# Relative-position attention on one core: query tile 0 split into two halves for the scores and the logits

## What is computed

```python
idx = clip(key - query, -64, 64) + 64
rk, rv = embK[idx], embV[idx]
q, k, v = proj(Wq, bq), proj(Wk, bk), proj(Wv, bv)          # 16 heads of 16
logits = einsum('bhqd,bhkd->bhqk', q, k) + einsum('bhqd,qkd->bhqk', q, rk)
w = softmax(logits, axis=-1)
out = einsum('bhqk,bhkd->bhqd', w, v) + einsum('bhqk,qkd->bhqd', w, rv)
y = out.reshape(nb, seq, 256) @ Wo.T + bo
x = x + layernorm(y)                    # the input of y is layernorm(x)
x = x + layernorm(layernorm(x) @ ternary(weight).T * alpha + bias)
```

## Time and profile before

| | |
|---|---|
| median of 3 runs | 2659.86 us |
| the three runs | 2678.59, 2659.86, 2657.63 us |
| the profiled execution, its own time | 2678.59 us |
| its span, first to last instruction | 2676.8 us |
| instructions | 100468 |
| TensorE busy | 2534.3 us, 95%, 42130 matmuls |
| VectorE, ScalarE, GpSimd busy | 2022.9 us (76%), 1553.2 us (58%), 969.2 us (36%) |
| mean granted TensorE clock | 0.938 of 2.4 GHz |

### The profile page before, as it was taken

One profiled execution on the slowest core, in us unless ns is written; L12 is line 12 of the kernel. 1 busy time (PEld: TensorE's weight loads), 2 busy tenths in 40 slices (PEclk: granted clock), 3 DMA queues, 4 the chain that ended last, 5 costly groups with the idle time before them and its releaser, 6 DMA issues.

```text
span 2676.8 us, 100468 instructions
## 1 busy us (share of the span) xinstructions
PE 2534.3 (95%) x42130; PEld 1959.7 (73%) x42130; DVE 2022.9 (76%) x5187; ACT 1553.2 (58%) x2993; POOL 969.2 (36%) x2275
## 2 busy tenths in 40 slices
PE   5899999999999999999999999999999999999994
PEld 4477777777777777777777777777777777777773
DVE  4777678876887778876788767887688777887774
ACT  2456665556565655565655566556666556666651
POOL 3114323433345333453244432444333533341026
PEclk8699999999999999999999999999999999999997
DMA  7656654556445564555645656456644556445410
GB/s 225 180 143 183 172 157 131 142 170 193 144 135 164 153 181 138 159 162 159 172 136 145 185 161 168 129 142 181 178 147 147 137 168 188 141 144 157 134 34 25
DMA packets 605039, 408.96 MB, mean 153 GB/s; under 512 B 149162, under 2 KB 604330, under 8 KB 604330
## 3 DMA queue, kind: packets, MB, share of 16 engines
q1 hardware_dynamic: 604586, 402.54, 52.6%
HBM read 206.84 MB, written 194.90 MB: 150 GB/s over the span
## 4 chain that ended last, share of the span: by engine, by line
PE 73%; DVE 16%; issue 4%; ACT 2%; POOL 2%; DMA 1%; SPq 0%; DVEq 0%; POOLq 0%; ACTq 0%
PE oacc L793 16%; PE logitsT L755 15%; PE scores L733 14%; PE logitsT L760 7%; DVE maxes L1012 6%; DVE junk L1009 6%; PE misc L856 4%; PE misc L690 4%; PE misc L806 3%; PE misc L818 2%; PE misc L707 2%; PE misc L830 2%; ACT wxr L1212 1%; PE misc L843 1%; DVE stats L915 1%
## 5 line engine op out<-in xcount | busy, mean ns | idle before, releaser
L1009 DVE CUSTOM_DVE_ANT_1 junk<-scores,bands 128x512 bf16<-128x512 f32 x988 | 679.4, 688 | 427.9 <-PE scores L733 408.9
L755 PE MATMUL logitsT<-qs,ks 98*128 98x128 bf16 (+1 forms) x8192 | 980.6, 221 | 20.0 <-ACT wxr L1212 13.2
L1212 ACT ACTIVATE wxr<-logitsT 128x512 f32<-128x512 f32 x1024 | 586.0, 605 | 419.4 <-PE logitsT L755 379.3
L1212 ACT ACTIVATE wy<-logitsT 128x512 f32<-128x512 f32 x1024 | 591.0, 598 | 402.3 <-PE logitsT L755 389.3
L755 PEld LDWEIGHTS logitsT<-qs,ks 98*128 98x128 bf16 (+1 forms) x8192 | 664.2, 99 | 212.2 <-issue 76.2
L733 PE MATMUL scores<-ks,qs 96*128 96x256 bf16 (+6 forms) x3712 | 681.7, 289 | 54.8 <-DVE maxes L1012 31.6
L1012 DVE TENSOR_REDUCE maxes<-scores 128x1 f32<-128x512 f32 x1024 | 702.3, 686 | 1.9 <-PE scores L733 1.9
L760 PE MATMUL logitsT<-ident,bands 128*128 128x128 f32 x2048 | 463.7, 278 | 0.0
L733 PEld LDWEIGHTS scores<-ks,qs 96*128 96x128 bf16 (+1 forms) x3712 | 287.8, 98 | 207.5 <-DVE maxes L1012 112.3
L1240 POOL TENSOR_SCALAR rs<-rs 128x1 int32<-128x1 int32 (+1 forms) x224 | 45.8, 204 | 822.5 <-DVE rs L920 811.9
L760 PEld LDWEIGHTS logitsT<-ident,bands 128*128 128x128 f32 x2048 | 292.4, 143 | 43.4
(11 more groups left out here) (136 smaller groups left out, 2638.3 us busy)
## 6 DMA issues: line engine op xcount, KB each, us to landing
bs<-praw SPq DMA_DIRECT2D x256, 512.0 KB, 3.7
bands<-bs SPq DMA_DIRECT2D x224, 512.0 KB, 4.8
ks<-kd SPq DMA_DIRECT2D x64, 384.0 KB, 4.5
qs<-qd SPq DMA_DIRECT2D x112, 192.0 KB
bands<-bs SPq DMA_DIRECT2D x128, 128.0 KB, 3.9
qd<-qparts SPq DMA_DIRECT2D x64, 192.0 KB, 3.0
kd<-kparts SPq DMA_DIRECT2D x64, 192.0 KB, 2.6
qd<-qparts SPq DMA_DIRECT2D x64, 128.0 KB, 2.4
```

What stands on the lines that cost most here:

```text
L755: mm = e.matmul(lt[:, c * P:(c + 1) * P], kk[0:depth, h, kt * P:(kt + 1) * P], qs[i][0:depth, h, :], start=True, stop=not near, skip_group ...
L1009: e.tensor_tensor_reduce(junk[:], scores[:, 0:512].rearrange("p (a c) -> p a c", a=2), banded, 1.0, LOWEST, ALU.add, ALU.max, mx[:, h, 0:1 ...
L1212: e.activation(dst, src, ACT.Exp).then_inc(exp_ready, 1)
```

## The change

Queries of tile 0 are treated as two halves in the scores and the logits. `sides(t, kt)` takes the place of `is_right`: for tiles other than 0 it gives one piece over all 128 queries, for tile 0 and key tile 0 one piece without far rows, and for tile 0 with any other key tile two pieces, queries 0 to 63 without the far rows and 64 to 127 with them. `score_pieces` gives pieces with their range of query rows; for tile 0 they are sorted by bank, then by first row, then by column. The far rows of the first half are no longer zero rows but the queries' own.

```diff
-def is_right(t, kt):
-
-
-    return kt > t
+def sides(t, kt):
+
+
+    if t:
+        return [(0, P, kt > t)]
+    if kt == 0:
+        return [(0, P, False)]
+    return [(0, HALF, False), (HALF, P, True)]
...
     for i, kt in enumerate(near_first(t)):
-        right = is_right(t, kt)
-        last = pieces[-1] if pieces else [0, 0, 0, None]
-        if P * i % 512 and last[3] == right and last[1] + last[2] == P * kt:
-            last[2] += P
-        else:
-            pieces.append([P * i, P * kt, P, right])
+        for r0, r1, right in sides(t, kt):
+            same = [x for x in pieces if x[3:] == [r0, r1, right] and x[0] + x[2] == P * i and x[1] + x[2] == P * kt]
+            if same and P * i % 512:
+                same[0][2] += P
+            else:
+                pieces.append([P * i, P * kt, P, r0, r1, right])
+    if t == 0:
+        pieces.sort(key=lambda x: (x[0] // 512, x[3], x[0]))
     return pieces
...
-                            late = src[rows, :, S - HALF:S]
-                            if rows.start:
-                                late = bass.AP(qd[b % 2].tensor, (g * ROWS + MAXROW) * HG * S, [[0, ROWS - SPLIT], [S, HG], [1, HALF]])
-                            e.dma_start(qs[i][rows, :, 0:HALF], late).then_inc(qs_in[i], 16)
+                            e.dma_start(qs[i][rows, :, 0:HALF], src[rows, :, S - HALF:S]).then_inc(qs_in[i], 16)
...
-                    for x, (c, key, length, right) in enumerate(pieces):
+                    for x, (c, key, length, r0, r1, right) in enumerate(pieces):
...
-                        mm = e.matmul(scores[:, c:c + length], qs[i][0:depth, h, :], kk[0:depth, h, key:key + length],
+                        mm = e.matmul(scores[r0:r1, c:c + length], qs[i][0:depth, h, r0:r1], kk[0:depth, h, key:key + length],
                                       start=True, stop=True, skip_group_check=True)
...
-                        depth = ROWS if is_right(t, kt) else FAR
-                        mm = e.matmul(lt[:, c * P:(c + 1) * P], kk[0:depth, h, kt * P:(kt + 1) * P], qs[i][0:depth, h, :],
-                                      start=True, stop=not near, skip_group_check=True)
+                        for q0, q1, right in sides(t, kt):
+                            depth = ROWS if right else FAR
+                            mm = e.matmul(lt[:, c * P + q0:c * P + q1], kk[0:depth, h, kt * P:(kt + 1) * P],
+                                          qs[i][0:depth, h, q0:q1], start=q0 == 0, stop=not near, skip_group_check=True)
```

## The result

| | before | changed |
|---|---|---|
| median of four executions | 2660.17 us | 2709.62 us (2708.95 to 2712.35) |
| ratio, 95% interval | | 1.0179 (1.016 to 1.0199) |
| span of the profiled execution | 2676.8 us | 2709.8 us |
| mean granted clock in it | 0.938 | 0.985 |

The change costs 49.5 us of the median, 1.0186 times the time before. The ratio in the table is that of the means of 4 and of 21 executions, and the 4 hold the one of 2678.59 us. Forecast were +50 us, 2710 us.

A forecast was written before the change was run, and what follows sets the result against it. TensorE's instruction stream was taken as the bound, VectorE close behind. Scores +49 us, logits +1 and the rest 0 made +50 us over the median 2659.86, so 2710 us, range 2674 to 2764.

The forecast's parts named there:

- What bounds: TensorE's instruction stream is the time, busy 95%; work added to it is paid nearly one for one.
- Part 1, price of a change: Tile 0 scores: four changes a head between whole array and half strips, 0.10 us each, 0.40 us together.
- Part 1, streaming: Tile 0 scores: halves run side by side, 1152 columns against 1024, +0.056 us a head.
- Part 1, what hides it: Tile 0 heads whose second bank waits for VectorE swallow some added time: 9 us taken, leaving +49 of +58.4 us.
- Part 2: Tile 0 logits: 7 more weight loads a head, nearly hidden behind 64-column matmuls, +1 us.
- Part 3: Far rows of tile 0's first 64 queries read from their own place; equal transfers, no added wait, 0 us.
- The sum: Whole kernel: 49 + 1 = +50 us, forecast 2710 us, +1.9%.
- Median and profiled execution: The +50 us is added to the median, 2659.86 us, not to the slowest, profiled execution of 2678.59 us.
- 1 (57 ns a pair): Logits: a 128-wide load cannot follow in 28 ns; total +100, 2760 us; 0.24 shared with the halves-in-sequence rival.
- 2 (halves one after the other): Tile 0 scores: halves don't run side by side, +43, 2753 us; chance 0.24 shared with the weight-load rival.
- 3 (changes cheap): Tile 0 scores: mode changes cheap or hidden, about 2668 us; chance 0.14 with partial prices up to 2685.
- 4 (clock): Whole kernel: TensorE holds clock 1.00 instead of 0.95, 22 us faster, 2638 us; chance 0.04.

The follow-up runs named there:

- e5: Changed kernel with the whole-array score matmul cut into two of 64 columns between halves, six mode changes a head: 2740.32 us, ratio 1.0296.
- e3: Changed kernel with the one whole-array score matmul moved ahead of the halves, two mode changes a head instead of four: 2683.11 us, ratio 1.0089.
- e1: Changed kernel with only the scores of tile 0 split, logits and far-row load as before the change: 2703.85 us, ratio 1.0172.
- e2: Changed kernel with only the logits of tile 0 split, scores and load as before the change: 2665.87 us, ratio 1.0026.
- e8: Changed kernel with the far-row load as before, zero rows for the first half of tile 0: 2710.4 us, ratio 1.0191.

## Why the prediction was right

- **What bounds.** Right for the 93 of 128 heads that don't wait: there TensorE's added time was paid one for one. e5 shows it at its purest, 29 us more than the change in the rows and 30.9 in the medians.
- **Part 1, price of a change.** Predicted 0.10 us each from the quarter strips; the half strips show 0.10, 0.13, 0.10, 0.10. The Trainium skill, TensorEngine Tiling (Array Packing), Key Properties, names the drain at a switch of tiling mode; the gaps in which neither matmul nor load begins, and e3, where two changes fewer are 0.23 us of a head, bear the rule out.
- **Part 1, streaming.** The halves run side by side, as forecast: 0.06 us between the starts of the two of 512 columns. Over 128 more columns of 0.05 us, some 0.03 us a head were not in the sum: the second matmul on a half after a change starts 27 ns late. A head cost 0.84 + 0.10 - 0.45 = 0.49 us more, not 0.456: 62 us gross, not 58.4. That the weight load of that second matmul can't be hidden is the likely cause; that was only argued.
- **Part 1, what hides it.** This term was mis-sized: 9 us predicted, 15 in the heads that wait. The count was nearly right, by luck: a quarter of the heads, from two of eight seen in one step. In that step there are three, the third without a bracket because its records merge, in most of the steps between there is one, and in all it is 35 of 128. What each of them hides was too low: 0.42 us of its 0.49, where "up to 0.35" was cut down to 9 / 32 = 0.28.
- **Part 2.** Mis-sized the other way: +1 predicted, +6.9 measured, with 32.5 ns a pair in place of the 28. The 1 ns over streaming seen at 128 columns did not hold at 64, where it is 5.8.
- **The sum.** The two errors cancel: +44.8 (e1) against the predicted +49, and +6.9 (e2) against +1. That the whole came within 1 us of the forecast is luck; that it lay in the range is not.
- **Part 3.** Right, e8.
- **Median and profiled execution.** The sum over the median was the right choice. Made against 2678.59 us it would have been off by 19.
- **Rivals.** 1 (57 ns a pair) fell by 32.5; 2 (halves one after the other) by 0.06 us between starts; 3 (changes cheap) by the four gaps, so the 8-wide transpose, which has no gap, was no guide to a 64-wide strip; 4 (clock) is out: the clock of the changed kernel is 0.985, and that of the kernel before 0.982 in the run beside it.

## What to carry to other kernels

Count the changes between whole-array and narrow matmuls, in both directions, and put matmuls of one width side by side: here 0.10 to 0.13 us each, and moving one matmul gave back 25.4 us of 49.5, about a fifth of it because two halves then ran side by side. But don't pull apart what keeps another engine fed: where TensorE is 95% busy and VectorE 76%, larger blocks that should have saved up to 18 us of changes made the kernel 34 us slower. And measure waiting heads start to start, over all steps, since merged rows hide short waits and the steps differ.

## What the runs showed that was not expected

- A profiled execution can lie at the slow end by its clock alone: 2676.8 us at a mean granted clock of 0.938 of 2.4 GHz, 2658.7 us at 0.982, the same kernel.
- Joining blocks of TensorE work with everything else alike made the kernel slower three times, by 4.7, 34 and 133 us, though each saved changes of mode.
